# Layer-0 causal attention: one full-height product for the maxima of four heads, and the context's norm moved beside the context attention

## The reference

```python
q, k, v = _heads(x @ Wq + bq), _heads(x @ Wk + bk), _heads(x @ Wv + bv)   # 16 heads of 16
att = einsum('bhqd,bhkd->bhqk', q, k) * scale
att = where(tril, att, -inf)                       # causal, 512 x 512
y = einsum('bhqk,bhkd->bhqd', softmax(att), v)
qc, kc, vc = heads(x @ Wcq + bcq), heads(ctx @ Wck + bck), heads(ctx @ Wcv + bcv)
y = y + einsum('bhqk,bhkd->bhqd', softmax(qc kc^T * scale), vc)            # full, 512 x 1024
x = x + y @ Wp + bp
# layer 1, later: yn = layernorm(ctx) * g + b ; k = yn @ wk ; v = yn @ wv
```

## Time and profile before

| | |
|---|---|
| runs | 1804.22, 1815.93, 1812.98 us; median 1812.98 |
| profiled execution | 1818.22 us, span 1816.5, mean granted clock 0.907 |
| TensorE busy | 1615.3 us, 89% |
| VectorE, ScalarE, GpSimd busy | 869.0, 687.3, 348.1 us |
| DMA | 84.29 MB, mean 46 GB/s |

### The profile page before, as it was taken

How to read it: one execution, slowest core, us unless ns; L and a number is a source line. 1 busy time by engine, 2 the same in 40 slices (tenths; PEclk the granted TensorE clock), 3 DMA queues, 4 the chain that set the end, 5 groups by cost and what they waited for, 6 DMA issues and landing times.

```text
span 1816.5 us, 24884 instructions
## 1 busy us (share of the span) xinstructions
PE 1615.3 (89%) x10159; PEld 820.6 (45%) x10159; DVE 869.0 (48%) x1881; ACT 687.3 (38%) x1022; POOL 348.1 (19%) x495
## 2 busy tenths in 40 slices
PE   8999989899999986799485899899899999995997
PEld 5788843222233335377254333356222222454565
DVE  2255456688645526310357347523666775202221
ACT  3443223666542232321141545542245555531111
POOL 2043143000012230300311113242101000213100
PEclk9999999999985558799688999999799999996999
DMA  5000010000000005734102100021300000092100
GB/s 184 1 1 1 1 50 0 1 1 1 1 1 1 1 1 201 248 121 136 51 1 38 16 1 1 24 72 56 110 1 1 1 1 24 1 360 71 51 10 11
DMA packets 70341, 84.29 MB, mean 46 GB/s; under 512 B 24945, under 2 KB 55889, under 8 KB 69202
## 3 DMA queue, kind: packets, MB, share of 16 engines
q1 hardware_dynamic: 67395, 75.31, 12.8%
q0 software_dynamic: 2832, 7.38, 1.3%
HBM read 63.56 MB, written 19.51 MB: 46 GB/s over the span
## 4 chain that ended last, share of the span: by engine, by line
PE 45%; DVE 6%; ACT 3%; DMA 2%; issue 2%; POOL 1%; SPq 0%; DVEq 0%; ACTq 0%; POOLq 0%
PE psum L1201 5%; PE psum L1171 5%; PE psum L2962 4%; PE psum L1191 4%; PE psum L1135 4%; PE psum L2298 3%; PE psum L2305 3%; PE psum L1904 3%; DVE a_nm L1241 3%; PE psum L1292 2%; PE psum L2983 2%; PE psum L1896 2%; PE psum L2288 2%; PE psum L1162 1%; PE psum L2313 1%
## 5 line engine op out<-in xcount | busy, mean ns | idle before, releaser
L1241 DVE TENSOR_REDUCE a_nm<-psum 128x1 f32<-128x512 f32 x384 | 249.1, 685 | 144.1 <-PE psum L1135 141.4
L1241 DVE TENSOR_REDUCE xa_nm<-psum 128x1 f32<-128x512 f32 (+3 forms) x384 | 226.3, 618 | 141.4 <-PE psum L1138 76.6
L1221 ACT ACTIVATE a_w<-psum 128x1024 f32<-128x1024 f32 x192 | 186.1, 1021 | 195.0 <-PE psum L1171 172.5
L1135 PE MATMUL psum<-a2kr,a2qr 32*128 32x512 bf16 x256 | 91.2, 404 | 15.1 <-DVE a_nm L1241 14.9
L1201 PE MATMUL psum<-a_w,ones 128*32 128x512 f32 x768 | 103.8, 613 | 0.5 <-ACT a_w L1221 0.5
L1162 PE MATMUL psum<-xa_mrow,onesb 3*128 3x512 bf16 (+3 forms) x384 | 68.5, 391 | 20.6 <-ACT xn L1221 7.4
L1221 ACT ACTIVATE xn<-psum 128x1024 f32<-128x1024 f32 (+3 forms) x64 | 55.6, 921 | 74.0 <-PE psum L1171 74.0
L1135 PEld LDWEIGHTS psum<-a2kr,a2qr 32*128 32x128 bf16 x256 | 20.1, 92 | 136.8 <-DVE a_nm L1241 121.9
L1171 PE MATMUL psum<-a2qT,a2kT 32*128 32x512 f32 x512 | 80.7, 612 | 0.0
L1171 PE MATMUL psum<-xa_cq,xa_ckT 32*128 32x512 f32 x512 | 80.5, 617 | 0.0
L1221 ACT ACTIVATE xnT<-psum 128x1024 f32<-128x1024 f32 (+3 forms) x64 | 54.8, 907 | 67.2 <-PE psum L1171 67.2
(11 more groups left out here) (508 smaller groups left out, 2951.2 us busy)
## 6 DMA issues: line engine op xcount, KB each, us to landing
mo_w<-in_L_ffn_W SPq DMA_DIRECT2D x16, 1024.0 KB, 8.2
sw_wv<-in_L_ffn_w_v SPq DMA_DIRECT2D x4, 2048.0 KB, 18.9
scratch_a2v<-co_v SPq DMA_DIRECT2D x16, 256.0 KB, 2.0
scratch_a2k<-co_k SPq DMA_DIRECT2D x16, 256.0 KB, 3.5
a2kT<-scratch_a2k SPq DMA_DIRECT2D x8, 512.0 KB, 8.4
a2v<-scratch_a2v SPq DMA_DIRECT2D x4, 1024.0 KB, 12.0
sw_wp<-in_L_ffn_w_proj SPq DMA_DIRECT2D x4, 1024.0 KB, 20.0
a1li<-in_L_xattn_a_li_w SPq DMA_DIRECT2D x2, 1024.0 KB, 6.1
```

The source lines that it names most:

```text
L1135: t = e.matmul(out[:, 0:N], query[:, chunk(i)], key[:, half * S:half * S + N], start=True, stop=not causal)
L1221: e.activation(self.w[s % 3][:, 2 * jj:2 * jj + 2, lo:S], ps[:, pr:pr + 2, lo:S], ACT.Exp, scale=self.scale).then_inc(*self.weighed.mark(n ...
L1241: e.tensor_reduce(self.nm[n % 3][:, q, half, h:h + 1], ps[:, self.pair_of("max", *i), 0:N], AX.X, ALU.max, negate=True).then_inc(*self.max ...
```

## The change

- The rounded keys of a causal job's four heads are spread into a tile `kb` of 128 partitions x 4 x 512: head h has its keys in rows 32h to 32h+31 of block h and zeros elsewhere. One product with all 128 rows of queries then gives the scores of 128 queries against the same 128 keys of four heads, a bank of 512. A causal job has 10 such products (i+1 for query chunk i) and, on the diagonal, 4 masks of 512 columns (`mask_four`). VectorE reduces a bank to four maxima (`parts`), and one small reduction at the end takes the largest over the chunks.
- The keys' rounding in the lead-in goes; GpSimd spreads them instead, 4 copies of 32 partitions per batch and half (batch 0 ahead of the attention's order, batch 1 after `max_parts` of jobs 9 and 11).
- In causal jobs the maxima are shared out over the chunks by their size. The division is its own step, one chunk after the inversion, in all four-head attentions.
- The context's norm: load first in the stage's DMA queue, all statistics on VectorE at the start of the lead-in, roots on ScalarE in the lead-in, scales on VectorE after it, the 16 normalisations on GpSimd before the attention's order.
- In `Moe`, SyncE issues the third expert's weights and the retention weights after six value stores.
- `mask_four` is made by four copies at the program's start; three tiles `parts` and two tiles `kb` are set in the lead-in.

```diff
@@ Norm.vector_apply, Norm.pool_apply
-        if self.gain is None:
+        if self.gain is None and "a" in self.split:
...
+                if self.gain is None:
+                    e.tensor_scalar(dst, self.src[:, c, :], self.agg[:, c, 0:1], self.std[:, c, 0:1], ALU.subtract, ALU.mult).then_inc(
+                        *self.by["p"].mark(self.name, c))
+                    continue
@@ FourHeads
+    def items(self, n):
+        if self.jobs[n].mode == "causal":
+            return [(n, i, j, 0) for i in range(SC) for j in range(i + 1)]
+        return [(n, i, half, h) for i in range(SC) for half in range(self.halves(n)) for h in range(4)]
...
                 at = each * (i + 1) * (count + 1) // count ** 2 if n == 0 else each * (i + 2) // count
+                if job.mode == "causal":
+                    sizes = [S - self.first_query(n, j) for j in chunks]
+                    at = math.ceil(each * (sum(sizes[:i + 1]) / sum(sizes) + 0.3))
...
-                        turns = [("turn_den", late[0]), ("invert", late[0])]
+                        turns = [("turn_den", late[0]), ("invert", late[0]), ("divide", late[0])]
@@ tensor_max
-        out, causal = self.k.ps[:, bank, :], job.mode == "causal"
-        N = (i + 1) * P if causal else S
-        t = e.matmul(out[:, 0:N], query[:, chunk(i)], key[:, half * S:half * S + N], start=True, stop=not causal)
-        if causal:
-            w.wait_ge(*self.k.const.made.at("masks"))
-            t = e.matmul(out[:, N - P:N], self.k.const.identb[:, :], self.k.const.mask_qk[:, :], start=False, stop=True)
+        if job.mode == "causal":
+            t = e.matmul(out, query[:, chunk(i)], key[:, :, chunk(part)], start=True, stop=part < i)
+            if part == i:
+                w.wait_ge(*self.k.const.made.at("masks"))
+                t = e.matmul(out, self.k.const.identb[:, :], self.k.const.mask_four[:, :, :], start=False, stop=True)
@@ vector_steps
+                    e.tensor_reduce(self.parts[n % 3][:, q, part, :], view.rearrange("p (h n) -> p h n", n=P), AX.X, ALU.max, negate=True).then_inc(
+                        *self.max_taken.mark(*i))
...
+                    e.tensor_reduce(nm[:, :, 0, :], self.parts[i % 3][:, :, :, :].rearrange("p i s h -> p i h s"), AX.X, ALU.min).then_inc(
+                        *self.max_taken.mark(i, "all"))
@@ CrossAttention
+        self.kb = [sb(f"kb{i}", [P, 4, S], BF16) for i in range(2)]
...
+            rounded = lambda h: (qr[odd][:, m, cols(b)], self.kb[m][:, :, :])
@@ sync_program
+        self.operands.sync_context(e)
@@ pool_program
-        self.attention.pool_steps(e, w, self.attention.order())
+        self.operands.pool_apply(e, w)
+        for m in range(FC):
+            self.pool_spread(e, w, 0, m)
+        for step, i in self.attention.order():
+            self.attention.pool_steps(e, w, [(step, i)])
+            if step == "max_parts" and i in (9, 11):
+                self.pool_spread(e, w, 1, i // 2 - 4)
+
+    def pool_spread(self, e, w, b, m):
+        w.wait_ge(*self.projections["k"].exact(m, b))
+        if b:
+            w.wait_ge(*self.attention.maxed.at(*self.attention.items(9 + 2 * m)[-1]))
+        for h in range(4):
+            rows = slice(32 * h, 32 * h + 32)
+            w.wait_ge(*self.k.pool.now())
+            e.tensor_copy(self.kb[m][rows, h, :], self.kT[rows, m, cols(b)]).then_inc(*self.spread.mark(b, m) if h == 3 else self.spread.mark(b, m, h))
@@ scalar_program, vector_program
+            if at == 5:
+                self.operands.scalar_roots(e, w)
...
-        self.operands.scalar_roots(e, w)
...
+        self.operands.vector_stats(e, w)
         w.wait_ge(self.loads["rows"].sem, 48)
...
-            if step == "invert" and 8 <= i < 12:
-                self.operands.vector_stats(e, w, 4 * (i - 8))
+        self.operands.vector_scales(e, w)
@@ ContextOperands
-        self.norm = Norm(k, "co_norm", self.rows, self.rows, "vaaa", chunks=MC, mem=mem)
+        self.norm = Norm(k, "co_norm", self.rows, self.rows, "pppp", chunks=MC, mem=mem)
@@ Moe
-        for x in range(3):
+        for x in range(2):
             self.load(e, w, x)
-        self.retention.sync_weights(e, w)
         for i in range(10):
+            if i == 7:
+                self.load(e, w, 2)
+                self.retention.sync_weights(e, w)
             self.operands.sync_step(e, w, i)
...
-        self.operands.scalar_apply(e, w)
...
-        self.operands.vector_apply(e, w)
```

More of the change, by code:

```diff
@@ L1 @@
+import math
 from contextlib import ExitStack
@@ L210, in pool_program @@
         w.wait_ge(*step.now())
+        for i in range(4):
+            e.tensor_copy(self.mask_four[:, i, :], self.mask_qk[:, :]).then_inc(*step.mark())
+            w.wait_ge(*step.now())
         e.tensor_copy(self.mask_kq[:, :], self.maskf[:, 1, :]).then_inc(*self.made.mark("masks"))
@@ L902, with __init__ @@
 class FourHeads:
-    def __init__(self, k, tag, owner, jobs, d, scale, mem, upper=False, weights=(), outs=()):
+    def __init__(self, k, tag, owner, jobs, d, scale, mem, upper=False, causal=False, weights=(), outs=()):
         self.k, self.tag, self.owner, self.jobs, self.d, self.scale, self.upper = k, tag, owner, jobs, d, scale, upper
@@ L929, in halves, with in_parts @@
         return self.jobs[n].keys // S
+    def in_parts(self, n):
+        return self.halves(n) == 2 or self.jobs[n].mode == "causal"
     def chunks(self, n):
@@ L938, in maxima @@
         for n in range(len(self.jobs)):
-            items = [(n, i, half, h) for i in range(SC) for half in range(self.halves(n)) for h in range(4)]
-            for j, item in enumerate(items):
+            for j, item in enumerate(self.items(n)):
                 yield "max", item
@@ L1008, in order @@
             yield "den", late
-        for step in ("settle", "turn_den", "invert"):
+        for step in ("settle", "turn_den", "invert", "divide"):
             yield step, late[0]
@@ L1046, in pool_set @@
             e.memset(t[:, :, :, :], 0.0).then_inc(*self.set.mark())
+        for t in self.parts:
+            w.wait_ge(*pool.now())
+            e.memset(t[:, :, :, :], -NEG).then_inc(*self.set.mark("parts"))
     def pool_steps(self, e, w, steps):
@@ L1369, in memory @@
         outs = [self.W[n][:, :, :].rearrange("p f n -> p (f n)") for n in ("Wq", "Wk", "Wcq", "Wv")]
-        self.attention = FourHeads(k, "xa", self, self.jobs, D // H, (D // H) ** -0.5, mem, weights=weights, outs=outs)
+        self.attention = FourHeads(k, "xa", self, self.jobs, D // H, (D // H) ** -0.5, mem, causal=True, weights=weights, outs=outs)
         x = lambda f, n: k.xnT[:, f, cols(n)]
@@ L1403, in job @@
         made = HeadJob(query, key, rounded, value, keys, "full" if cross else "causal", b, (m, odd),
-                       lambda: [pq.done(m, b)] + [pk.done(m, n) for n in parts], lambda: [pq.exact(m, b)] + [pk.exact(m, n) for n in parts])
+                       lambda: [pq.done(m, b)] + ([pk.done(m, n) for n in parts] if cross else [self.spread.at(b, m)]), lambda: [pq.exact(m, b)] + [pk.exact(m, n) for n in parts])
         made.cross = cross
@@ L1541, in vector_program @@
                 self.attention.vector_steps(e, w, [(step, i)])
-        for step, i in self.attention.order():
-            self.attention.vector_steps(e, w, [(step, i)])
-            if step == "invert" and 8 <= i < 12:
-                self.operands.vector_stats(e, w, 4 * (i - 8))
+        self.operands.vector_scales(e, w)
+        self.attention.vector_steps(e, w, self.attention.order())
         for c in range(NC):
```

72 lines of the change are left out of this document (44 added, 28 removed).

## The result

The change makes the kernel faster: the median of four executions is 1762.44 us (1758.42 to 1763.63), that of the kernel before on the same chip 1809.62 (1804.22 to 1815.93, four), ratio 0.9734, 95% interval 0.9694 to 0.9774. The profiled execution took 1758.42 us (span 1756.7, granted clock 0.946), 59.8 us less than that of before.

A forecast was written before the change was run, and what follows sets the result against it. TensorE at half clock bounds the layer-0 causal cross attention. -52.6 (seven causal jobs), -2, -2, -2, +2, -5 sum to -61.6 us: 1818.22 profiled to 1756.6, 1752 against the median; own range 1742 to 1767.

The forecast's parts named there:

- Seven causal jobs: Layer-0 cross attention: jobs fall from 19.5 to 12.0 us each, nearly all at full clock, gaining 52.6 us.
- The loop's own sum: Causal job's loop of scores, exponentials and next chunk's ranks: pairs of 1.94, 1.5, 1.1, 0.66 plus waits make 11.1 us.
- the reason for the clock: Causal stage: small or 32-row products hold the clock at 0.50; full-height products bring it to 1.00 for nearly all.
- Price of a change of height: TensorE: going between a 32-row product and a 128-row one costs about 0.10 us, at full or half clock.
- third rival: TensorE mode changes cost more; at 0.6 us each the kernel is slower, 1847 us; chance of slower 0.03.
- second rival: VectorE becomes the causal jobs' bound, 15 us each, total 1773; chance 0.18, shared with an up-and-down clock.
- GpSimd: Norms and first spreads done at 328 to 340 us, later spreads of 2.5 us behind maxima already taken: cost nothing.
- Last job: Last causal job of the cross attention: from 11.2 us to about 9, a gain of 2 us.
- Maxima of jobs 8 and 9: Inside cross jobs 6 and 7: product and mask in ScalarE's wait fall from 0.47 us to 0.41 or nothing, gaining 2.
- Tail and output: Tail's output products after the causal jobs no longer start at half clock: a gain of 2 us.
- Lead-in: Cross attention's start: context statistics on VectorE move the first reduction from 250.00 to 251.8, a loss of 2 us.
- Expert lead-in: Experts' search and stores: a TensorE stall of 5.93 us goes, key chain may be pushed back; gain 5, bounds 2 to 8.

The follow-up runs named there:

- run 10: Kernel before with only the context norm's new place and the value stores moved; products, order, division as before: 1799.49 us, ratio 0.9869, over four fastest of ten.
- run 12: The kernel of run 1 (32-row products per head) without the causal maxima's masks, so part of the computation is left out: 1742.26 us, ratio 0.9636.
- run 9: Kernel before with only the new products (spread keys, parts, four-fold mask); order, norm, division and stores as before: 1766.95 us, ratio 0.9782.
- run 2: Changed kernel with sixteen products and masks per causal job, one per head, each product 128 rows high against spread keys: 1761.94 us, ratio 0.9717.
- run 1: Changed kernel with the causal maxima's old products put back (32 rows, per head, mask each), all else kept: 1778.65 us, ratio 0.9815.
- run 4: Kernel before, unchanged, profiled once more: 1813.31 us.
- run 6: Changed kernel with the maxima given evenly to the steps of a causal job, as before: 1759.35 us, ratio 0.974.
- run 7: Changed kernel with GpSimd's division back at the inversion's place, a step earlier: 1760.78 us, ratio 0.9748.
- run 8: Changed kernel with second-batch spread copies one by one behind four cuts, and third expert's weights loaded behind the sorted rows: 1751.84 us, ratio 0.9692.
- run 11: Changed kernel with per-head products, heads 1 and 3 taking 128 rows, heads 0 and 2 their 32: 1764.94 us, ratio 0.9756.
- run 3: Kernel before with each causal mask product as wide as its product, 3,072 more columns per causal job: 1804.13 us, ratio 0.9965.

## Why the prediction was right, and where not

The time is inside the own range (1742 to 1767); 1752 was 10 us too low, the sum against the profiled executions 1.8 too high in gain (61.6 against 59.8). Term by term:

- **Seven causal jobs**, forecast 52.6, measured 136.6 - 86.8 = 49.8. 12.0 us a job was right but for the job of 15.8. That it would be nearly all clock was right, and more so than I had it: run 10 has the old job at full clock at 12.50 us, so seven would be 87.5 and the clock 49 of the 49.8. The loop's own sum in the prediction, 5.2 us of exponentials and four waits from 1.7 down to 1.4, makes 11.4 and not 11.1, which moves the low end of the range by 2 us.
- **The step that failed is the reason for the clock**: "the clock is at 0.50 where small or 32-row products make up most of the time and 1.00 where full ones do". Run 12 has mostly 32-row products and 1.00. I wrote that I am wrong if the clock there is not set by what part of the array works; by run 12 it is not, at least not by that alone. The rows read before could have told: a cross job has 32 maxima products of 32 rows, 0.31 us each, 9.9 of its 24.3 us of TensorE, and ran at 1.00:
```profile
416.75:443.13 26.38, 24.32 (x196) 6.96 (x196) 22.30 (x38) 15.99 (x18) 2.26 (x5) 1.00 0.00 1
```
  That the clock came back as forecast is therefore partly luck. The new products did bring it back (run 9 against before, run 2 against run 1), but no run shows why. They also took TensorE's work from 12.50 us a job to 11.2, just below what the job takes, and that is common to all kernels that stayed up.
- What the profiles show in its place is an association, and a loose one. With the old products TensorE has no pause of its own in a full-clock job (runs 1, 4 and 10). It was busy 35.88 of 35.88 us ahead of the fall at 568.5 (run 1), 13.12 of 13.12 in the job that ended 1 us ahead of the fall at 541.5 (run 4), and 42.50 of 42.50 ahead of that at 572.5 (run 10):
```profile
530.00:572.50 42.50, 42.50 (x388) 16.89 (x380) 30.66 (x66) 19.67 (x31) 17.61 (x30) 1.00 0.01 1
```
  Once at half, the old job fills TensorE again, 21.00 of 21.00. In the kernels that stayed up to about the last job but one (after apart from the job of 15.8, 2, 6, 7, 8, 9, 11, 12) most jobs leave TensorE idle for 0.3 to 1.3 us: 0.46 of 12.01 in run 2, 1.03 of 9.88 in run 12. Against a rule made of this: the first two jobs of after are idle for only 0.10 and 0.13 us and did not fall; TensorE waits often, 20.53 of 23.50 us busy, in the stretch of layer 1 at 0.50; and run 3 idles 1.5 us in jobs that are mostly at 0.50.
- Other falls came 1 to 2 us after a wait of 0.9 to 1.2 for VectorE (before, runs 3, 4 and 5), but the falls of run 1 at 585.5 and 602.5 had no wait ahead of them, and run 2 has a wait for GpSimd and no fall:
```profile
565.74 0.85 PE L1217 MATMUL psum<-xnT,xa_v 128*32 128x384 f32 x8 [1.06 <-POOL xnT L1079]
```
  The Trainium skill (TensorE: Matmul & The Clock Gate, Part 1) says that busyness lifts the clock; the full stretches at 0.50 speak against it as the whole story. **What brings the clock down in a stage that never pauses stays open.** Run 1 with a short pause put into each job would tell; it wasn't tried.
- **Price of a change of height**, 0.10 us: held. TensorE in run 2 (tall product, mask, then scores of 32 rows), and after (tall product, four-fold mask, rank):
```profile
588.59 0.28 PE L1160 MATMUL psum<-xa_kb,xa_qr 128*128 128x256 bf16 x1
588.71 0.22 PE L1162 MATMUL psum<-mask_qk,identb 128*128 128x128 bf16 x1
588.86 0.71 PE L1197 MATMUL psum<-xa_q,xa_kT 32*128 32x256 f32 x8
```
```profile
588.09 0.39 PE L1161 MATMUL psum<-xa_kb,xa_qr 128*128 128x512 bf16 x1
588.32 0.38 PE L1164 MATMUL psum<-mask_four,identb 128*128 128x512 bf16 x1
588.63 0.40 PE L1190 MATMUL psum<-xa_mrow,onesb 3*128 3x512 bf16 x4
```
  From tall product to mask 0.12 us for 256 columns and 0.23 for 512, their columns and no more; from mask to 32-row or 3-row work 0.15 for 128 columns and 0.31 for 512, 0.10 on top. It also explains why run 2's jobs hold less work than run 1's (TensorE 11.55 us against 12.70): a tall product and its mask have the same height. The third rival needed 0.4 more.
- **VectorE** (second rival): the reduction to four maxima costs what one of 512 does, 685 ns in the mean of 60 against 692, the small one 263 ns. VectorE was busy 7.6 to 9.8 us in jobs 8 to 13, below TensorE's 10.5 to 12.7.
- **GpSimd**: ahead of job 0's division the norms took 16 x 0.87 and the spreads 8 x 0.66 us, and 13.38 idle were left: nothing, as forecast. "The later spreads: nothing" was wrong: 4.2 us, from the wait and the fall of the clock behind it (run 8's job is 11.6 instead of 15.8).
- **Last job** 2, measured 11.2 - 8.15 = 3.1. **Maxima of jobs 8 and 9** 2 gained; measured a loss of 1.2 (57.2 to 58.5 us for jobs 6 and 7): run 9, products alone, has 58.3, and runs 4 and 10, with the old products and order, 57.2, so the new products cost there; which part of them was not measured apart. **Tail and output**: 2, measured 22.3 - 19.6 = 2.7.
- **Lead-in**, loss of 2: first reduction 251.52 (251.8 forecast); job 7 settled 2.7 later, 1.2 of it the line above. Another 0.9 lies ahead of the stage and is not the change's: the products that turn its input start at 236.98 in after, 236.13 in before, and 237.00 in before again (run 4). About 0.6 is left for the lead-in itself, against 2 forecast.
- **Expert lead-in** 5, bounds 2 to 8: measured 73.5 - 70.8 = 2.7. The key chain took what the search gained, as the lower bound had it.
- **Not forecast**: 4.3 us behind the experts' start. The division does not give it (run 7), and runs 3 and 5, which are the kernel before in that part, have 1042.7 and 1037.9. It moves from profile to profile; why was not traced.
- **Against the median**: 61.6 was measured at 59.8 between profiled executions but 47.2 between medians. I scaled the sum by 5.2 us; the executions of before differ by more, 1804.22 to 1815.93 and 1818.22 profiled. Its two profiles fall at different moments in this stage.
- **The parts do not add up.** By ratio, products alone give 39 us, order alone 10, norm alone 24 (by medians, the safer number there, 12), order, norm and division together 33, all 48. The parts seem to buy some of the same clock; the mechanism is not shown.

## What to carry to other kernels

When a stage stands at half clock with the engine full, price its work at full clock first: if a job is 12.5 us there and 21.0 here, the clock is the prize, and several small edits may each win the same part of it, so test them alone and together before crediting one. Put work that TensorE may have to wait behind (statistics, spreads) where the stage has slack, and copies for a later batch one at a time behind the cuts, never ahead of them. A mask on a maximum that only shifts the softmax can cost more than it looks: with it gone here, narrow products ran beside each other and the job lost 3.9 us of TensorE's work for 2.6 us of masks; leaving it out changes what is computed (the shift is then the largest score of a whole diagonal block, which could underflow rows whose allowed scores are all far below), so that has to be argued for the data. The best full version here is run 8; its combination with run 12 was not run.

## What the runs showed that I had not expected

- The granted clock went to 0.50 with TensorE busy 42.50 of 42.50 us ahead of it, and stayed there while it was busy 21.00 of 21.00.
- More work did not cost time: 3,072 more columns in each of eight jobs, ratio 0.9965 (0.9938 to 0.9991).
- Taking out masks of 0.16 us each gained 36 us against the same kernel with them (1778.65 to 1742.26), in the profiles 35.8 in the eight jobs and 8.9 ahead of them; by full-clock jobs (12.70 to 9.88) it would be some 23 of the 35.8, and the rest is clock.
- With the statistics ahead of it, the lead-in has a wait of TensorE for VectorE near 252: 0.24 us in after and runs 6 and 8, where the clock stayed up, 0.99 us in runs 1, 2, 10 and 11, where it was at 0.50 for 10 to 13 us from 252 to 255 on and job 0 settled 3.8 to 5.5 us later than in after. But run 12 has the same 0.99 us and no fall. A wait of one size is not enough to tell.
